# Where a masked prefix scan reads its mask: SBUF rows written by ScalarE, or six features in a PSUM bank written by VectorE

## The chip, the core and the metric

The kernel runs on one NeuronCore of a Trainium2 chip. The metric is the time of one execution on the device in microseconds (us), the median of several runs. TensorE (PE in the profile; PEld is its weight load), VectorE (DVE), ScalarE (ACT), GpSimd (POOL) and SyncE (SP) are the engines. GpSimd issues the indirect DMAs, SyncE and ScalarE issue the plain ones.

## What is computed

A node state x of 12500 rows with 32 features goes through four graph layers. Each layer reads, for every one of 400000 edges, the row of the source node, turns it into a message of 32 features, adds up the messages of each destination node, adds the result to x and normalizes:

```python
edge_index = jnp.stack([src, dst])
...
x = _layernorm(x + _L3_gnn_ref(x, edge_weight, edge_attr_3, edge_index, ...w1, b1, w2, b2), axis=-1)

def _L3_gnn_ref(features, abs_distances, rel_vec, edge_index, w1, b1, w2, b2):
    R = jax.nn.relu(abs_distances[:, None] @ w1 + b1) @ w2 + b2
    Y = spherical_harmonics(rel_vec)
    Fj = features[src]
    ...  # acc += NORM * einsum('euv,ef,evi,ofi->euo', R, Y, Fj, C)
    out = out.at[dst].add(msg)
```

The edges are sorted by destination. So the sum per destination is made as a running sum along the edges that is set back to zero wherever the destination changes: `so[t] = mask[t] * so[t-1] + si[t]`, with a mask of zeros and ones. The last value of every run of equal destinations is the sum of that node.

## The kernel before

Each of the 128 partitions holds 3125 consecutive edges, worked through in 125 chunks of T = 25 edges. The last layer (L3) runs in `vector_edges3`, `scalar_edges3`, `tensor_edges3`, `gpsimd_edges3` and `sync_edges3`, one software pipeline in which every engine has its own hand-written order and waits on counters of the others. The body of a loop holds four chunks, because rows that are gathered have four buffers.

What happens to one chunk c:

- GpSimd (L1937) gathers the source rows, 25 indirect DMAs of one row per partition each, into one of four buffers `gb`. It waits until SyncE's index load is there and until VectorE has begun chunk c-4 (`mA0`).
- VectorE turns the vector part of the gathered rows into the edge's frame with three products `al0`, `al1`, `al2` (L1047), one chunk ahead; TensorE adds the three up with identity matmuls (`along`, L1743) into the PSUM area `L3.rot`, columns 2728 to 3328 of all PSUM, that is from column 168 of bank 5 into bank 6. ScalarE copies the result out (`scalar_split3`, L1427 to L1431).
- TensorE makes the edge's radial weights, 384 numbers per edge, in ten groups of three and two edges: `radial(g)`, L1756. VectorE multiplies each group with the rotated features in two instructions, `mA{g}` and `mB{g}` (L1077 and L1080 for groups 0 to 2, L1087 and L1090 for groups 3 to 9). Groups 0 to 2 are added up by TensorE (`over_v`, L1783), groups 3 to 9 by VectorE (`r3` to `r9`, L1099). `radial(g)` waits for `mB{g-2}`, since its PSUM banks are read by it; so `radial(2)` waits for `mB0`, and `radial(0)` and `radial(1)` of the next chunk for `mB8` and `mB9`. A product waits for its `radial`.
- In the following chunk the sums are turned back: VectorE `bk0`, `bk1`, `bk2` (L1053), TensorE `back` (L1743) into the same `L3.rot`, ScalarE copies them into the scan's input `si` (`scalar_vectors3`, L1443) and counts that in `ac_B`. `si` is stored feature by feature, 32 rows of 26: the first of the 26 is the carried value of the last chunk, copied by ScalarE (L1437), then 25 edges.
- VectorE scans (`sc`, L1156): one instruction over 832 elements per partition, with the mask `L3.mrf`, the same 26 values repeated for the 32 features, as its first input and `si` as its second. Both are in SBUF. The mask row is written by ScalarE once per chunk (L1466, 800 elements), the first column of each 26 is zero from the start (L1161).
- ScalarE turns the scan's output around (`scalar_row3`, L1457) and stores it; then it copies the sums of `over_v` (L1449, L1450), and only after that the split of the next chunk. TensorE's `along(0)` waits for L1450.

The order on VectorE is written out as a list of names; the counter `dv` counts them, and all waits on VectorE are made from the list (`v3(c, name)`). The names in `BACK3` belong to the previous chunk. TensorE's order is radial 0, 1, 2, back 0, radial 3, 4, back 1, radial 5, back 2, radial 6, over_v 0 and 1, radial 7, over_v 2 and 3, radial 8, along 0 and 1, radial 9, along 2. ScalarE's order in a chunk is L1437, L1438, L1466, L1414, L1443, L1420, L1457, L1449, L1450, L1427 to L1431.

Layers 0 and 2 use the same scan on 832 elements, with the mask in PSUM (L847 and L1009); their gathers are L1955 and L1977.

Of the kernel before, what the change touches and what calls it, by code (L numbers as in the profile page):

```python
# [9 lines left out]
ALU = mybir.AluOpType  # L10
ACT = mybir.ActivationFunctionType
# [3 lines left out]
P = 128  # L15
TP = E // P
NP, NJ = 125, 100
T = 25
# [48 lines left out]
def gnn_kernel(nc, x, src, dst, ea2, ea3, ea5, ew, ew1, W0, W1, G2, MU, SG, ROOT, BIAS, w1, b1, w2, b2, out):  # L67

    ctx = ExitStack()
    with ctx:  # L70
        ctx.enter_context(nc.allow_non_contiguous_dma(reason="small strided loads of weights and block heads"))

        def sb(name, shape, dt=F32):
            return ctx.enter_context(nc.sbuf_tensor("s_" + name, shape, dt))
# [6 lines left out]
        def sem(name):  # L81
            if name not in sems:
                sems[name] = ctx.enter_context(nc.semaphore("m_" + name))
            return sems[name]
# [14 lines left out]
        mask = sb("mask", [P, TP])  # L99
# [48 lines left out]
        ps = [psall[:, 512 * i:512 * i + 512] for i in range(8)]  # L148

        dv = Count(sem("dv"))  # L150
        idle = sem("idle")
        idle2 = sem("idle2")
        mk = {}
# [20 lines left out]
        r3 = lambda a: a[0:NP, :].rearrange("p (j c) -> p j c", c=32)  # L174
# [4 lines left out]
        cv = Carve()  # L179
        dsti, dstf, q2 = cv(TP, I32), cv(TP), cv(TP)  # L180
        cv = Carve(17900)
# [12 lines left out]
        for layer in (0, 2):  # L194
            cv = Carve(15400 if layer == 0 else 0)
# [4 lines left out]
        cv = Carve(10350)  # L200
# [23 lines left out]
        cv = Carve()  # L224
# [12 lines left out]
        cv = Carve()  # L237
# [28 lines left out]
        cv = Carve()  # L266
# [19 lines left out]
        cv = Carve()  # L286
# [11 lines left out]
        cv = Carve(21400)  # L298
# [10 lines left out]
        cv = Carve()  # L309
# [22 lines left out]
        cv = Carve()  # L332
        L3 = Layer()
# [2 lines left out]
        L3.fr = [cv(T * 9) for _ in range(2)]  # L336
        L3.HS = [cv(P * T) for _ in range(2)]
        L3.ds = [cv(P * T) for _ in range(2)]
        L3.sif, L3.sof, L3.mrf = ([cv(32 * (T + 1)) for _ in range(2)] for _ in range(3))
        L3.si, L3.so, L3.mr = ([a.rearrange("p (f t) -> p f t", f=32) for a in b] for b in (L3.sif, L3.sof, L3.mrf))  # L340
        L3.sit = [a[:, :, 1:T + 1].rearrange("p f t -> p t f") for a in L3.si]
        L3.row = [cv(32 * T), agg[:, 1800:2600]]
        L3.prod = [cv(3 * 512).rearrange("p (t c) -> p t c", t=3) for _ in range(2)]
# [670 lines left out]
        def vector_edges2(e):  # L1014
# [12 lines left out]
            for k in range(B2):  # L1027
# [3 lines left out]

        ORDER = ("mA0 mB0 mA1 mB1 bk0 mA2 mB2 bk1 mA3 mB3 bk2 mA4 mB4 r3 mA5 mB5 r4 al0 mA6 mB6 r5 sc al1 "
                 "mA7 mB7 r6 al2 mA8 mB8 r7 mA9 mB9 r8 r9").split()
        PER3 = len(ORDER)
        AT3 = {name: n + 1 for n, name in enumerate(ORDER)}
        BACK3 = ("bk0", "bk1", "bk2", "sc")

        def v3(c, name):  # L1040

            return c * PER3 + (mk["base3"] + AT3[name])
# [13 lines left out]
        def vector_chunk3(e, c, i, k, first=False, last=False):  # L1056
            s2, p2 = k % 2, (k - 1) % 2
            R = psall[:, :].rearrange("p (b c) -> p b c", c=512)
            done = lambda name: e.wait_ge(dv.h, v3(c, name))
            done_before = lambda name: e.wait_ge(dv.h, v3(c - 1, name))  # L1060

            def skip(name):
                done(ORDER[AT3[name] - 2])
                e.sem_inc(dv.up(1), 1)

            def prod(g):
                return L3.prod[ONDVE.index(g) % 2][:, 0:GROUPS[g][1]]

            def mul(g):
                t0, n = GROUPS[g]  # L1070
                Rg = R[:, BANK[g]:BANK[g] + n]
                if g == 0:
                    e.wait_ge(sem("ac_G"), c + 1)
                    e.wait_ge(sem("pe_v"), c + 1)
                e.wait_ge(sem("pe_r"), c * 10 + (g + 21))
                if g in ONPE:
                    e.tensor_tensor(  # L1077
                        L3.prodA[:, t0:t0 + n], Rg[:, :, 0:256].rearrange("p t (v b) -> p t v b", v=16),
                        L3.G[s2][:, t0:t0 + n].unsqueeze(3).to_broadcast([P, n, 16, 16]), ALU.mult).then_inc(dv.up(), 1)
                    e.tensor_tensor(  # L1080
                        L3.prodE[:, 2 * t0:2 * (t0 + n)], Rg[:, :, 256:384].unsqueeze(2).to_broadcast([P, n, 2, 128]),
                        L3.GE[s2][:, t0:t0 + n].rearrange("p t a v -> p (t a) v").unsqueeze(3).to_broadcast([P, 2 * n, 16, 8]), ALU.mult).then_inc(dv.up(), 1)
                    return
                pr = prod(g)
                m = ONDVE.index(g)
                done(f"r{ONDVE[m - 2]}") if m > 1 else done_before(f"r{ONDVE[6 - m]}")
                e.tensor_tensor(  # L1087
                    pr[:, :, 0:256].rearrange("p t (b v) -> p t b v", v=16), Rg[:, :, 0:256].rearrange("p t (b v) -> p t b v", v=16),
                    L3.G[s2][:, t0:t0 + n].unsqueeze(2).to_broadcast([P, n, 16, 16]), ALU.mult).then_inc(dv.up(), 1)
                e.tensor_tensor(  # L1090
                    pr[:, :, 256:512], Rg[:, :, 256:384].unsqueeze(2).to_broadcast([P, n, 2, 128]),
                    L3.GE[s2][:, t0:t0 + n].rearrange("p t a v -> p (t a) v").unsqueeze(2).to_broadcast([P, 2 * n, 8, 16]), ALU.mult).then_inc(dv.up(), 1)

            def red(g):
                t0, n = GROUPS[g]
                done(f"mB{g}")
                if g == ONDVE[0]:
                    e.wait_ge(sem("ac_B"), c + 1)
                e.tensor_reduce(L3.sums[s2][:, t0:t0 + n].rearrange("p t c -> p (t c)"),  # L1099
                                prod(g).rearrange("p t (b v) -> p (t b) v", v=16), AX.X, ALU.add).then_inc(dv.up(), 1)  # L1100

            def along(j):
                if last:
                    skip(f"al{j}")
                    return
                if j == 0:
                    e.wait_ge(sem(f"g3_{(k + 1) % 4}"), nth4(i, k + 1) * 400)
                    e.wait_ge(sem("ac_M"), c + 2)
                    e.wait_ge(sem("pe_a"), c + 1)
                along3(e, k + 1, j).then_inc(dv.up(), 1)  # L1110

            def back(name):
                if first:
                    skip(name)
                else:
                    vector_back3(e, c, k, name)

            mul(0)
            mul(1)
            back("bk0")  # L1120
            mul(2)
            back("bk1")
            mul(3)
            back("bk2")
            mul(4)
            red(3)
            mul(5)
            red(4)
            along(0)
            mul(6)  # L1130
            red(5)
            back("sc")
            along(1)
            mul(7)
            red(6)
            along(2)
            mul(8)
            red(7)
            mul(9)
            red(8)  # L1140
            red(9)

        def vector_back3(e, c, k, name):

            s2, p2 = k % 2, (k - 1) % 2
            if name in ("bk0", "bk1", "bk2"):
                if name == "bk0":
                    e.wait_ge(dv.h, v3(c - 1, "r9"))
                    e.wait_ge(sem("ac_V"), c + 1)
                    e.wait_ge(sem("pe_b"), c + 1)  # L1150
                back3(e, k - 1, int(name[2])).then_inc(dv.up(), 1)
            else:
                e.wait_ge(dv.h, v3(c - 1, "sc"))
                e.wait_ge(sem("ac_B"), c + 2)
                e.wait_ge(sem("rowc3"), c)
                e.tensor_tensor_scan(L3.sof[p2], L3.mrf[p2], L3.sif[p2], 0.0, ALU.mult, ALU.add).then_inc(dv.up(), 1)  # L1156

        def vector_ready3(e):
            for a in range(2):
                e.memset(L3.sof[a], 0.0).then_inc(dv.up(), 1)  # L1160
                e.memset(L3.mr[a][:, :, 0:1], 0.0).then_inc(dv.up(), 1)  # L1161

                e.memset(L3.HS[a][64:128], 0.0).then_inc(dv.up(), 1)
                after(e)
                e.memset(L3.HS[a][64:65], 1.0).then_inc(dv.up(), 1)
            after(e)

        def vector_edges3(e):
# [16 lines left out]
            n = 0  # L1185
            for name in BACK3:
                e.wait_ge(dv.h, mk["base3"] + 125 * PER3 + n)
# [275 lines left out]
        def scalar_chunk3(e, c, i, k, first=False, last=False):  # L1463
            if not first:
                scalar_part3(e, c, k)
            e.activation(L3.mr[k % 2][:, :, 1:T + 1], mask[:, bass.ds(c * T, T)].unsqueeze(1).to_broadcast([P, 32, T]), ACT.Copy)  # L1466
            if not last:
                scalar_hidden3(e, i, k + 1, c + 1)
            if not first:
                scalar_vectors3(e, c, k)  # L1470
            if not last:
                e.wait_ge(dv.h, v3(c, "bk2"))
                scalar_frames3(e, i, k + 1)
            if not first:
                scalar_row3(e, c, i, k)
            scalar_sums3(e, c, k)
            if not last:
                scalar_split3(e, c + 1, k + 1)
# [786 lines left out]
```

## Time and profile before

| | us |
|---|---|
| median of 3 runs | 17409.68 |
| lowest and highest run | 17409.63 to 17410.06 |
| profiled execution | 17404.72 |
| its span, first to last instruction | 17402.7 |

One execution is profiled, all engines at once. The busy time of an engine is the sum of its instructions; a row of the timeline gives the start, the duration and, in square brackets, how long the engine was idle before it and what released it. Where several instructions of one line follow each other they stand in one row with xN. PEclk is the granted clock of TensorE as a share of 2.4 GHz; behind it stand the share of the DMA engines and GB/s. Because successive instructions of VectorE overlap a little, the distance from start to start is what one instruction costs in a row of them, and it is a little less than its duration. The last layer's loop takes about 4050 us of the span, from 13184 to 17240.

### The profile page before, as it was taken

To read this page: it belongs to the slowest core of one execution; us is meant where nothing else is said; L and a number is where in the kernel's file an instruction comes from. 1 tells how busy PE (TensorE), PEld (TensorE's weight loads), DVE (VectorE), ACT (ScalarE), POOL (GpSimd) and SP (SyncE) were. 2 spreads that over 40 slices of the span, in tenths; PEclk is the share of its full clock that TensorE was granted. 3 is DMA by queue.
4 is the path that set the end of the run, shared out by engine and by line. 5 is a ranking of instruction groups with operands and counts; after the bars stand their busy time and mean duration, and the time that the engine had idled before them with its cause. 6 is when DMAs were issued, how large, how long until landed. Compare 5 with 4: busy or idle time off the path is not lost. (4 is left out here: it accounts for less than half of the span.)

```text
span 17402.7 us, 138752 instructions
## 1 busy us (share of the span) xinstructions
PE 6419.3 (37%) x33487; PEld 5142.6 (30%) x33487; DVE 12117.7 (70%) x15588; ACT 3285.1 (19%) x5336; POOL 12932.6 (74%) x13715
## 2 busy tenths in 40 slices
PE   1000000000444454545330000000006999999995
PEld 0000000000333333333320000000005878878774
DVE  5666666674899999999663232223326999999996
ACT  0000000000222222222541101111102223222321
POOL 6777777777677777777757777777777777777776
PEclk9555555555777777777665555555558999999998
DMA  4333333331111111111332222222222222222221
GB/s 103 97 96 97 97 98 97 98 97 47 28 28 28 28 28 28 28 28 25 130 130 59 59 57 59 58 59 58 59 53 45 55 55 53 56 53 56 53 56 36
DMA packets 744244, 1076.69 MB, mean 62 GB/s; under 512 B 375703, under 2 KB 508493, under 8 KB 731294
## 3 DMA queue, kind: packets, MB, share of 16 engines
q0 software_dynamic: 417376, 477.82, 12.5%
q1 hardware_dynamic: 250851, 398.14, 8.2%
q10 hardware_dynamic: 75736, 197.70, 3.1%
q8 instruction: 88, 1.44, 0.0%
q14 instruction: 193, 1.58, 0.0%
HBM read 684.92 MB, written 389.48 MB: 62 GB/s over the span
## 5 line engine op out<-in xcount | busy, mean ns | idle before, releaser
L1937 POOL DMA_INDIRECT s_arena<-d_t,s_arena x3125 | 3086.5, 988 | 971.3 <-issue 943.6
L1898 POOL DMA_INDIRECT d_pay<-s_arena x3125 | 3026.9, 969 | 997.7 <-issue 931.0
L1977 POOL DMA_INDIRECT s_arena<-d_t,s_arena x3125 | 2960.6, 947 | 1032.6 <-issue 952.0
L1955 POOL DMA_INDIRECT s_arena<-d_t,s_arena x3125 | 2948.5, 944 | 981.7 <-issue 952.1
L1649 PE MATMUL psall<-s_arena 128*128 128x500 bf16 x1875 | 835.4, 500 | 4365.4 <-DVE psall L881 3637.1
L992 DVE TENSOR_TENSOR s_arena<-s_arena,psall 128x2400 f32<-128x2400 f32 x125 | 332.0, 2656 | 2712.1 <-DMA s_arena<-d_t,s_arena 2712.1
L1649 PEld LDWEIGHTS psall<-s_arena 128*128 128x128 bf16 x1875 | 222.5, 119 | 4783.3 <-DVE psall L881 3708.7
L1756 PE MATMUL psall<-s_w2r,s_arena 128*128 128x384 f32 x4250 | 1514.0, 491 | 5.9 <-DVE s_arena L1090 5.2
L1838 PE MATMUL psall<-s_tails,s_mfix 128*128 128x32 f32 x6 | 1.9, 412 | 3972.8 <-DVE s_tails L1198 3972.8
L1756 PEld LDWEIGHTS psall<-s_w2r,s_arena 128*128 128x128 f32 x4250 | 1271.0, 317 | 64.3 <-DVE s_arena L1090 6.1
L1099 DVE TENSOR_REDUCE s_arena<-s_arena 128x64 f32<-128x1024 f32 x875 | 1248.1, 1438 | 0.0
L1838 PEld LDWEIGHTS psall<-s_tails,s_mfix 128*128 128x128 f32 x6 | 1.5, 313 | 3974.0 <-DVE s_tails L1198 3974.0
L1666 PE MATMUL psall<-s_ident,s_arena 128*128 128x128 f32 x3125 | 603.3, 321 | 1406.8 <-DVE s_arena L665 1406.8
L1675 PE MATMUL psall<-s_arena 128*128 128x128 f32 x6250 | 1052.1, 316 | 112.3 <-ACT s_arena L1360 103.5
L901 DVE TENSOR_REDUCE s_arena<-s_arena 128x600 f32<-128x4200 f32 x125 | 1027.2, 8218 | 4.3
L1360 ACT ACTIVATE s_arena<-psall 128x512 f32<-128x512 f32 x875 | 482.7, 552 | 2743.3 <-PE psall L1666 2743.3
L1675 PEld LDWEIGHTS psall<-s_arena 128*128 128x128 f32 x6250 | 906.0, 221 | 309.7 <-DVE s_arena L688 150.6
L564 DVE TENSOR_TENSOR s_arena<-s_arena,psall 128x625 bf16<-128x625 f32 x1250 | 957.7, 801 | 0.0
L890 DVE TENSOR_TENSOR s_arena<-s_arena,psall 128x600 f32<-128x600 f32 x125 | 97.5, 780 | 1172.4 <-DMA s_arena<-d_t,s_arena 1172.4
L1783 PE MATMUL psall<-s_arena,s_ident 128*128 128x256 f32 x4000 | 907.4, 378 | 0.0
L1666 PEld LDWEIGHTS psall<-s_ident,s_arena 128*128 128x128 f32 x3125 | 451.9, 168 | 1430.0 <-issue 1430.0
L1512 ACT ACTIVATE s_arena<-s_arena 128x800 f32<-128x800 f32 x125 | 213.9, 1711 | 3492.9 <-DVE psall L864 3463.7
(304 smaller groups left out, 17923.9 us busy)
## 6 DMA issues: line engine op xcount, KB each, us to landing
s_arena<-d_t,s_arena POOLq DMA_INDIRECT x9375, 2.5
d_scan<-s_arena ACTq DMA_DIRECT2D x313, 400.0 KB, 2.6
s_arena<-d_ew SPq DMA_DIRECT2D x126, 800.0 KB
s_arena<-d_pay SPq DMA_DIRECT2D x33, 1650.0 KB, 6.8
d_inj<-s_agg SPq DMA_DIRECT2D x125, 400.0 KB, 3.9
s_arena<-d_inj SPq DMA_DIRECT2D x125, 400.0 KB, 3.4
d_pay<-s_arena POOLq DMA_INDIRECT x3125, 2.2
d_fold<-s_arena ACTq DMA_DIRECT2D x33, 1250.0 KB, 4.9
```

The lines of the kernel that those rows point to most:

```text
L564: return e.tensor_tensor(O[sl], h5[:, :, bass.ds(n, 1)].to_broadcast([P, 5, 125]), iob, ALU.is_equal)
L901: e.tensor_reduce(S[:, :, 8:32], w7.rearrange("p m t c -> p t c m"), AX.X, ALU.add)
L1099: e.tensor_reduce(L3.sums[s2][:, t0:t0 + n].rearrange("p t c -> p (t c)"), prod(g).rearrange("p t (b v) -> p (t b) v", v=16), AX.X, ALU.ad ...
L1649: e.matmul(R5s[:, 0:4], lhsT, rhs[:, 0:4], start=start, stop=True, skip_group_check=True)
L1666: m = e.transpose(ps[6][:, 128 * t:128 * t + 128], S1.xb[:, 128 * (t0 + t):128 * (t0 + t) + 128], ident[:, :])
L1675: m = e.matmul(ps[2 + yb][:, 128 * t:128 * t + 128], S1.xT[yb][:, 128 * t:128 * t + 128], S1.wt, start=True, stop=True)
L1756: m = e.matmul(ps[BANK[g] + t][:, 0:384], hv_[:, :, t0 + t], L3.w2v if g in ONPE else w2r[:, :], start=True, stop=True)
L1783: m = e.matmul(L3.vs, ident[:, :], L3.prodP[:, v], start=v == 0, stop=v == 15, skip_group_check=True)
L1898: e.indirect_dma_start(pay_d, bass.IndirectOffsetOnAxis(ap=S1.adr[s4][:, t:t + 1], axis=0), S1.pay[s4][:, 33 * t:33 * t + 33], None).then_ ...
L1937: e.indirect_dma_start(L3.gb[s][:, t], None, T3_d, bass.IndirectOffsetOnAxis(ap=L3.idx[s][:, t:t + 1], axis=0)).then_inc(sem(f"g3_{s}"), 16)
L1955: e.indirect_dma_start(L0.gb[s][:, t * 128:(t + 1) * 128], None, T0_d, bass.IndirectOffsetOnAxis(ap=L0.idx[s][:, t:t + 1], axis=0)).then_i ...
L1977: e.indirect_dma_start(L2.gb[k][:, t * 96:(t + 1) * 96], None, T2_d, bass.IndirectOffsetOnAxis(ap=L2.idx[k][:, t:t + 1], axis=0)).then_inc ...
```

## The change

VectorE gets a new step `mk`, placed ahead of `r4`. It copies the 25 mask values of the chunk, repeated for six features, from SBUF into columns 0 to 155 of PSUM bank 5, which nothing used. The mask of ScalarE (L1466) and both SBUF mask buffers are gone. The scan `sc` becomes six instructions, five of 156 elements and one of 52, each with the same PSUM mask; it moves from behind `r5` to ahead of `al0`. The wait on `ac_B`, which stood at `sc`, now stands at `mk`. For the first chunk there is a memset of the six zero columns instead of `mk`.

```diff
-        L3.sif, L3.sof, L3.mrf = ([cv(32 * (T + 1)) for _ in range(2)] for _ in range(3))
+        L3.sif, L3.sof = ([cv(32 * (T + 1)) for _ in range(2)] for _ in range(2))
+        L3.mrf = ps[5][:, 0:6 * (T + 1)]
+        L3.mr = L3.mrf.rearrange("p (f t) -> p f t", f=6)
...
-        ORDER = ("mA0 mB0 mA1 mB1 bk0 mA2 mB2 bk1 mA3 mB3 bk2 mA4 mB4 r3 mA5 mB5 r4 al0 mA6 mB6 r5 sc al1 "
+        ORDER = ("mA0 mB0 mA1 mB1 bk0 mA2 mB2 bk1 mA3 mB3 bk2 mA4 mB4 r3 mA5 mB5 mk r4 sc al0 mA6 mB6 r5 al1 "
                  "mA7 mB7 r6 al2 mA8 mB8 r7 mA9 mB9 r8 r9").split()
-        BACK3 = ("bk0", "bk1", "bk2", "sc")
+        BACK3 = ("bk0", "bk1", "bk2", "mk", "sc")
...
             mul(5)
+            if first:
+                e.wait_ge(sem("ac_B"), c + 2)
+                e.memset(L3.mr[:, :, 0:1], 0.0).then_inc(dv.up(), 1)
+            else:
+                back("mk")
             red(4)
+            back("sc")
             along(0)
             mul(6)
             red(5)
-            back("sc")
             along(1)
...
-            else:
+            elif name == "mk":
+                at = (c - 1) * T
+                m = mask[:, at:at + T] if isinstance(c, int) else mask[:, bass.ds(at, T)]
                 e.wait_ge(dv.h, v3(c - 1, "sc"))
                 e.wait_ge(sem("ac_B"), c + 2)
+                e.tensor_copy(L3.mr[:, :, 1:T + 1], m.unsqueeze(1).to_broadcast([P, 6, T])).then_inc(dv.up(), 1)
+            else:
+                e.wait_ge(dv.h, v3(c, "mk"))
                 e.wait_ge(sem("rowc3"), c)
-                e.tensor_tensor_scan(L3.sof[p2], L3.mrf[p2], L3.sif[p2], 0.0, ALU.mult, ALU.add).then_inc(dv.up(), 1)
+                for f in range(0, 32, 6):
+                    a, b = f * (T + 1), min(f + 6, 32) * (T + 1)
+                    m = e.tensor_tensor_scan(L3.sof[p2][:, a:b], L3.mrf[:, 0:b - a], L3.sif[p2][:, a:b], 0.0, ALU.mult, ALU.add)
+                m.then_inc(dv.up(), 1)
...
-            e.activation(L3.mr[k % 2][:, :, 1:T + 1], mask[:, bass.ds(c * T, T)].unsqueeze(1).to_broadcast([P, 32, T]), ACT.Copy)
```

## Rows read from the trace of the kernel before

**Rows 1.** Stretch: us, busy (count) of PE, PEld, DVE, ACT, POOL; PEclk.

```profile
15000.00:16000.00 1000.00, 941.10 (x3286) 800.74 (x3285) 944.59 (x1054) 298.74 (x434) 764.33 (x774) 0.98 0.25 55
```

**Rows 2.** Gathers of layers 3 and 2: calls, busy us, mean ns, idle.

```profile
L1937 POOL DMA_INDIRECT s_arena<-d_t,s_arena x3125 | 3086.5, 988 | 971.3 <-issue 943.6
...
L1977 POOL DMA_INDIRECT s_arena<-d_t,s_arena x3125 | 2960.6, 947 | 1032.6 <-issue 952.0
```

**Rows 3.** Timeline: one scan, and the gather that starts beside it.

```profile
15021.93 1.88 DVE L1156 TENSOR_TENSOR_SCAN s_arena<-s_arena 128x832 f32<-128x832 f32 x1
...
15022.22 2.35 POOL L1937 DMA_INDIRECT s_arena<-d_t,s_arena  x1 [0.30 <-issue]
```

**Rows 4.** VectorE's timeline of one undisturbed chunk, mA0 to the next mA0.

```profile
15003.96 0.95 DVE L1077 TENSOR_TENSOR s_arena<-psall,s_arena 128x768 f32<-128x768 f32 x1
...
15008.20 0.96 DVE L1077 TENSOR_TENSOR s_arena<-psall,s_arena 128x768 f32<-128x768 f32 x1 [0.54 <-PE psall L1756]
...
15016.73 1.74 DVE L1099 TENSOR_REDUCE s_arena<-s_arena 128x96 f32<-128x1536 f32 x1
...
15023.73 0.76 DVE L1047 TENSOR_TENSOR s_agg<-s_arena,psall 128x600 f32<-128x600 f32 x1
...
15027.26 0.77 DVE L1047 TENSOR_TENSOR s_agg<-s_arena,psall 128x600 f32<-128x600 f32 x1
...
15031.35 0.69 DVE L1087 TENSOR_TENSOR s_arena<-psall,s_arena 128x512 f32<-128x512 f32 x1 [0.38 <-PE psall L1756]
...
15035.34 0.95 DVE L1077 TENSOR_TENSOR s_arena<-psall,s_arena 128x768 f32<-128x768 f32 x1
```

**Rows 5.** Timeline, ScalarE and TensorE: L1443, along 2, radial 2.

```profile
15015.78 1.35 ACT L1443 ACTIVATE s_arena<-psall 128x600 f32<-128x600 f32 x1 [7.33 <-PE psall L1743]
...
15031.06 1.17 PE L1743 MATMUL psall<-s_agg,s_ident 128*128 128x344 f32 x4
...
15037.21 1.52 PEld L1756 LDWEIGHTS psall<-s_ta,s_arena 128*128 128x128 f32 x5 [2.22 <-DVE s_arena L1080]
```

**Rows 6.** Waits in the whole loop: us in total, times, longest.

```profile
ACT s_arena L1443 <- PE psall L1743: 985.1, 125, 10.3
...
DVE s_agg L1047 <- DMA s_arena<-d_t,s_arena: 57.7, 27, 8.5
```

**Rows 7.** Two successive mA0, and a stretch between them.

```profile
14615.64 0.95 DVE L1077 TENSOR_TENSOR s_arena<-psall,s_arena 128x768 f32<-128x768 f32 x1
...
14648.71 0.95 DVE L1077 TENSOR_TENSOR s_arena<-psall,s_arena 128x768 f32<-128x768 f32 x1
...
14619.00:14623.00 4.00, 4.00 (x9) 2.56 (x9) 2.46 (x4) 1.12 (x1) 3.09 (x4) 0.61 0.08 12
```

**Rows 8.** Two copies into PSUM, layer 2's scan, a short scan.

```profile
2030.06 0.23 DVE L863 COPY psall<-s_arena 128x75 f32<-128x75 f32 x1
2030.20 0.20 DVE L864 COPY psall<-s_arena 128x50 f32<-128x50 f32 x1
...
L1009 DVE TENSOR_TENSOR_SCAN s_arena<-psall,s_arena 128x832 f32<-128x832 f32 x125 | 236.6, 1892 | 23.2 <-DVE s_arena L949 4.8 <-DVE s_arena L956 4.6 <-DVE s_arena L972 4.6
...
L581 DVE TENSOR_TENSOR_SCAN s_arena<-s_arena 128x125 f32<-128x125 f32 x1 | 0.4, 420 | 0.0
```

**Rows 9.** The loop's last scan, and the copy it waits for.

```profile
17238.61 1.32 ACT L1443 ACTIVATE s_arena<-psall 128x600 f32<-128x600 f32 x1 [5.02 <-PE psall L1743]
17240.02 1.89 DVE L1156 TENSOR_TENSOR_SCAN s_arena<-s_arena 128x832 f32<-128x832 f32 x1 [4.31 <-ACT s_arena L1443]
```

**Rows 10.** mA0 of chunk 1 and of chunk 124.

```profile
13223.38 0.95 DVE L1077 TENSOR_TENSOR s_arena<-psall,s_arena 128x768 f32<-128x768 f32 x1
...
17201.71 0.95 DVE L1077 TENSOR_TENSOR s_arena<-psall,s_arena 128x768 f32<-128x768 f32 x1
```

**Rows 11.** First and last of 14 gaps over 2.4 us at radial 2.

```profile
13225.24 1.27 PEld L1756 LDWEIGHTS psall<-s_ta,s_arena 128*128 128x128 f32 x4 [2.64 <-DVE s_arena L1080]
...
17203.58 1.84 PEld L1756 LDWEIGHTS psall<-s_ta,s_arena 128*128 128x128 f32 x6 [2.94 <-DVE s_arena L1080]
```

More of the change, by code:

```diff
@@ L338, in gnn_kernel @@
         L3.ds = [cv(P * T) for _ in range(2)]
-        L3.sif, L3.sof, L3.mrf = ([cv(32 * (T + 1)) for _ in range(2)] for _ in range(3))
-        L3.si, L3.so, L3.mr = ([a.rearrange("p (f t) -> p f t", f=32) for a in b] for b in (L3.sif, L3.sof, L3.mrf))
+        L3.sif, L3.sof = ([cv(32 * (T + 1)) for _ in range(2)] for _ in range(2))
+        L3.si, L3.so = ([a.rearrange("p (f t) -> p f t", f=32) for a in b] for b in (L3.sif, L3.sof))
+        L3.mrf = ps[5][:, 0:6 * (T + 1)]
+        L3.mr = L3.mrf.rearrange("p (f t) -> p f t", f=6)
         L3.sit = [a[:, :, 1:T + 1].rearrange("p f t -> p t f") for a in L3.si]
@@ L1160, in vector_ready3 @@
                 e.memset(L3.sof[a], 0.0).then_inc(dv.up(), 1)
-                e.memset(L3.mr[a][:, :, 0:1], 0.0).then_inc(dv.up(), 1)
                 e.memset(L3.HS[a][64:128], 0.0).then_inc(dv.up(), 1)
```

## The prediction

> **What bounds the kernel now.** I went from the stretches to the timeline of one chunk, and from there to the waits. In the middle of the loop TensorE is busy for 94.1% and VectorE for 94.5% of the time, ScalarE for 30% [rows 1]. GpSimd shows 76%, but it never rests: its gathers are 0.30 us apart ("issue") and wait for nobody. So three engines are nearly full, and the change touches two of them.
>
> GpSimd: a gather takes 0.94 us plus 0.30, so 25 of them take about 31.2 us. In layer 3 the mean is 988 ns, in layer 2 it is 947 [rows 2]; 3125 x 41 ns = 128 us of extra. It sits in one place: of the 123 gathers longer than 1 us, 122 lie at a scan. The gather that starts 0.29 us after the scan takes 2.35 us and ends 0.76 us behind it [rows 3]. Layer 2's scan, equally long but with its mask in PSUM, lengthens none. The Trainium skill, "SBUF — State Buffer", section "Who interferes with whom", says that a VectorE instruction with two SBUF inputs holds up a GpSimd instruction that reads SBUF. The trace agrees, by those 122.
>
> TensorE and VectorE: an undisturbed chunk takes 31.38 us from mA0 to mA0 [rows 4]. VectorE is idle twice in it, 0.54 us before mA2 and 0.38 us before mA9, both times for TensorE. TensorE is idle once, 2.22 us, before radial 2, which waits for mB0 [rows 5]. So the loop goes: mB0, then TensorE without a break from radial 2 to radial 9, then VectorE alone with mA9, mB9, r8, r9, mA0, mB0. From mA2 to mA9 VectorE has 0.38 us to spare, not more.
>
> The measured mean is higher: 3978.33 us for 123 chunks [rows 10], 118.6 us above 123 x 31.38 = 3859.7. Two things make it up. After some of the gaps TensorE runs at the lower of its two clocks for a few us: one chunk takes 33.07 us, 1.69 more, with PEclk at 0.61 in a stretch of 4 us in it [rows 7], that is at 1.2 GHz for most of the stretch. I count 42 such starts in 124. The waits bear it out: L1443 waits 7.33 us in the undisturbed chunk [rows 5] and 985.1 in all [rows 6]; less the longest of 10.3, and less 124 x 7.33, that leaves 66 us, or 39 times 1.69. 42 x 1.69 = 71 us. The other 47.6 us are chunks in which al0 waits for the gathered rows (57.7 us in 27 waits, the longest of them ahead of these chunks [rows 6]).
>
> **Part by part.**
> - *ScalarE loses L1466 (0.89 us).* Worth nothing: behind it ScalarE waits 7.33 us for TensorE at L1443 [rows 5].
> - *The wait on ac_B moves up to mk.* L1443 ends at 15015.78 + 1.35 = 15017.13 [rows 5]; at the loop's end the scan starts 0.09 us after that copy is done [rows 9]. So mk starts at 15017.22 where r4 started at 15016.73 [rows 4]: 0.49 us of VectorE standing still. L1443 is fixed by TensorE's back 2, which doesn't move. Behind the wait stand r4, sc, al0 and everything up to mA9. At sc, 5 us later, the same wait cost nothing.
> - *mk, 150 elements, SBUF to PSUM.* The copy of 75 elements costs 0.14 us from start to start [rows 8]; 75 more, at mA2's 0.96 us less the overlap for 768 elements [rows 4], add 0.09. I take 0.22 us. Bounds: 0.14, and 0.31 if it doesn't overlap.
> - *Six pieces for one scan.* The scan of 832 takes 1.88 us, and 1.80 from start to start [rows 3, 4]. Between 125 elements (0.420) and 832 (1.892) [rows 8] an element costs 2.08 ns, which leaves 0.07 us fixed from start to start, or 0.15 as a duration. Five more pieces: 0.33 us, between 0 and 0.75. The mask in PSUM adds 0.01 (1.892 against 1.882).
> - *The pages price the pieces higher.* The trace shows an overlap of 0.08 us between the scan and al1 [rows 3, 4]. The Trainium skill, "VectorE: DVE Perf Modes", section "The DRAIN you can't avoid", says that the next instruction doesn't start until the pipe is empty, and advises few instructions. By that the pieces cost five full fixed parts; that is the high end above, and a rival below.
> - *sc and mk ahead of al0, mA6, mB6, r5.* al0 comes 0.49 + 0.22 + 2.14 = 2.85 us later, al1 and all behind it 1.05 us later. TensorE has room: al2 ends at 28.03, after the change at 29.1, and along 2 starts at 31.06 [rows 4, 5]; radial 8 and radial 9 have more. ScalarE's L1457 starts some 2.6 us earlier, which helps only where al0 waited for gathers.
> - *GpSimd's stall goes.* 31.2 us a chunk instead of 32.3. Alone it cannot give more than the 47.6 us of gather waits.
> - *SyncE, the DMAs issued and the start of the loop* stay. The tail, where mk and scan stand behind L1443, gets 0.6 us longer.
>
> **The sum.** VectorE gets 0.49 + 0.22 + 0.34 = 1.05 us between mA2 and mA9, has 0.38 to spare, and so mA9, and with it mB0 and the next radial 2, come 0.67 us later: 123 x 0.67 = 82 us. With a chunk now at 32.0 us or more and gathers at 31.2, the gather waits go: 47 us less. And TensorE's gap grows from 2.22 to 2.9 us. The gaps over 2.4 us that the trace has are 14 [rows 11], and after 7 of them the clock fell; of the 110 others 35 did. From 0.32 at 2.22 us and 0.5 at about 2.56 (most of the 14) a straight line gives 0.67 at 2.9: 83 starts instead of 42, 41 x 1.69 = 69 us. In all 82 - 47 + 69 + 1 = 105 us. The profiled execution took 17404.7 (span 17402.7); that gives 17510, and since the median of the runs is 5 us above the profiled one, 17515.
>
> **The rivals.**
> 1. *The clock falls no oftener.* Then 82 - 47 + 1 = 36 us, 17446 (each rival's time likewise against the median). For it: rows 11 are few. Against it: their share is above that of the short gaps. Chance 0.14; it lies on the border between no change and slower.
> 2. *VectorE pays each piece in full, or nearly every start runs slow.* Pieces at 0.15: 0.49 + 0.31 + 0.76 = 1.56, less 0.38 is 1.18, times 123 = 145; the clock falls in nearly all, 80 x 1.69 = 135; less 47: 233 us, 17643. The page named above would have it so for the first half. Against it: all rows of VectorE overlap. Chance 0.14.
> 3. *Faster: the added work fits into the spare time.* If mk does not have to wait and the pieces cost nothing, VectorE gets 0.22 to 0.38 us, mA9 stays where it is, and GpSimd's freed port shows in full: 47 us less, 17363. The place is mA9; the point from which it decides is an addition of 0.38 us. With mk unhindered but the pieces at 0.33 the addition is 0.56, the loop 0.18 longer, the clock a few times slower: 22 - 47 + 20, no change. For it: three causes of lost time (port, ScalarE, late scan) are truly taken away. Against it: mk's wait ends by TensorE's order. Chance 0.12 for faster, 0.08 for the middle.
> 4. *The gathers are still held up,* by mk instead of the scan, since it too reads SBUF. Layer 0's copies into PSUM (L863, L864) lengthen no gather. It would hardly show: 32.3 us of GpSimd is still below the 33 of the loop. No time of its own.
>
> **How the numbers follow.** Forecast 0.52, rival 1 0.14, rival 2 0.14, rival 3 and its middle 0.20. About 0.2% (35 us) is what a measurement can tell: faster means below 17375, slower above 17445. Faster 0.12; no change 0.08 plus half of rival 1, 0.15; slower the rest, 0.73. The forecast's own range, with mk at 0.14 to 0.31 us and 0.5 to 0.85 of the starts slow, is 17471 to 17563: 73 us for VectorE and 34 for 62 starts at the low end, 93 and 106 (105 starts) at the high end, less 47, plus 1. For eight in ten the range goes from 17390, leaving out only rival 3's faster part, to 17620, leaving out the end of rival 2.
>
> **What would show it.** In the profile of the changed kernel: gathers of layer 3 at a mean of 944 to 947 ns; GpSimd waiting for VectorE's mA0 (chunk c-4), which it never did; no DMA wait at al0 after the first chunks; mk idle 0.4 to 0.5 us for L1443; pieces 0.39 us apart; no idle before mA9; TensorE's gap at radial 2 of 2.9 us; undisturbed chunks of 32.0 us, slow ones of 33.7, and PEclk in the loop at 0.96 rather than 0.98. The forecast is wrong if mk starts at once, if mA9 still waits for TensorE, or if the gap grows and the slow starts don't.

## The result and the profile after

The changed kernel takes 17545.83 us (median of 4 runs, 17545.06 to 17549.53) against 17409.72 us of the kernel before on the same chip: a ratio of 1.0078, interval 1.0066 to 1.0090, 136 us slower. The profiled execution takes 17545.06 us, its span is 17543.0. The forecast was 105 us slower.

The middle of the loop by stretch, with the columns of [rows 1]:

```profile
15000.00:16000.00 1000.00, 928.49 (x3178) 780.58 (x3179) 926.44 (x1198) 262.52 (x388) 704.85 (x748) 0.96 0.25 53
```

All engines are less busy than before, and TensorE's mean clock is 0.96 instead of 0.98. The gathers, the pieces and the copy as groups:

```profile
L1950 POOL DMA_INDIRECT s_arena<-d_t,s_arena x3125 | 2948.6, 944 | 1216.5 <-issue 918.6
...
L1170 DVE TENSOR_TENSOR_SCAN s_arena<-psall,s_arena 128x156 f32<-128x156 f32 x620 | 243.2, 458 | 0.0
L1164 DVE COPY psall<-s_mask 128x150 f32 x120 | 38.2, 318 | 56.6 <-ACT s_arena L1457 56.6
```

A gather now takes 944 ns instead of 988 [rows 2], so the time that the scan took from GpSimd is gone (3086.5 - 2948.6 = 138 us). mk waited 56.6 us in 120 times, 0.47 us each. (L1457 is the copy that was L1443; L1769 is `radial`, L1756 the turns, L1079 and L1082 mA and mB of groups 0 to 2, L1089 those of the others.) The waits of the loop:

```profile
PEld psall L1769 <- DVE s_arena L1082: 366.4, 125, 3.6
...
POOL s_arena L1950 <- DVE s_arena L1089: 167.7, 61, 4.3
...
DVE s_arena L1079 <- issue: 14.2, 29, 0.7
DVE s_agg L1049 <- DMA s_arena<-d_t,s_arena: 8.4, 1, 8.4
```

GpSimd, which never waited, now waits (the line above alone is 167.7 us). The view names VectorE, since GpSimd waits on two semaphores there and VectorE's counter moved last. The timeline shows that the other one, SyncE's load of the chunk's indices, is what GpSimd waits for:

```profile
15015.37 0.34 SPq L2119 DMA_DIRECT2D s_arena<-in_src  x1
...
15022.26 0.94 POOL L1950 DMA_INDIRECT s_arena<-d_t,s_arena  x1 [2.30 <-DVE s_arena L1089]
```

The gather starts 6.89 us after the load was issued. From chunk 5 on the first gather of a chunk comes late 107 times, and each time it starts 6.4 to 8.1 us after its index load, while the mA0 of chunk c-4 lies more than 55 us back. SyncE in turn issues the load only after a wait for ScalarE (L1434, 123 times, 31.6 us each). So GpSimd is paced by the loop through ScalarE and SyncE, and not through its four buffers.

VectorE's waits for gathers have gone from 27 to the one at the start [rows 6]. TensorE's gap at radial 2 is 366.4 / 125 = 2.93 us in the mean. One line is new: VectorE stands still before mA0 in 29 chunks, for nothing that the profile shows. One undisturbed chunk on the timeline:

```profile
15011.81 1.36 ACT L1457 ACTIVATE s_arena<-psall 128x600 f32<-128x600 f32 x1 [9.86 <-PE psall L1756]
...
15012.16 0.68 DVE L1092 TENSOR_TENSOR s_arena<-psall,s_arena 128x512 f32<-128x512 f32 x1
15013.32 0.32 DVE L1164 COPY psall<-s_mask 128x150 f32 x1 [0.48 <-ACT s_arena L1457]
15013.54 1.74 DVE L1101 TENSOR_REDUCE s_arena<-s_arena 128x96 f32<-128x1536 f32 x1
...
15015.20 2.12 DVE L1170 TENSOR_TENSOR_SCAN s_arena<-psall,s_arena 128x156 f32<-128x156 f32 x6
...
15017.24 0.75 DVE L1049 TENSOR_TENSOR s_agg<-s_arena,psall 128x600 f32<-128x600 f32 x1
...
15027.97 0.69 DVE L1089 TENSOR_TENSOR s_arena<-psall,s_arena 128x512 f32<-128x512 f32 x1
...
15033.83 1.66 PEld L1769 LDWEIGHTS psall<-s_ta,s_arena 128*128 128x128 f32 x5 [2.81 <-DVE s_arena L1082]
```

The instruction ahead of r4 in the chunk of [rows 4], mB5, was this one:

```profile
15016.14 0.68 DVE L1090 TENSOR_TENSOR s_arena<-psall,s_arena 128x512 f32<-128x512 f32 x1
```

mk starts 0.15 us after L1457 is done. The bracket gives 0.48 us of idle time, but from start to start mB5 to mk takes 1.16 us where mB5 to r4 took 0.59, so the wait costs 0.57 us: the overlap of two instructions is lost with it. mk costs 0.22 us from start to start; the six pieces take 2.04 us from start to start where one scan took 1.80 [rows 3, 4]; mA9 (15027.97) no longer waits; and TensorE's gap is 2.81 us where it was 2.22 [rows 5]. The slow start that follows it is the rule now. The first and the last mA0 of the 123 chunks of [rows 10]:

```profile
13226.50 0.95 DVE L1079 TENSOR_TENSOR s_arena<-psall,s_arena 128x768 f32<-128x768 f32 x1
...
17339.21 0.95 DVE L1079 TENSOR_TENSOR s_arena<-psall,s_arena 128x768 f32<-128x768 f32 x1
```

That is 4112.7 us, 134.4 more than before. An undisturbed chunk takes 31.97 us (0.59 more), a slow one 33.65; 98 of 123 are slow. The sum: 123 x 0.59 = 73 us, 56 more slow starts x 1.68 = 94, the new stops 14, less the 48 us of gather waits: 133.

### The profile page after: what moved, and what is told of

Read it like the earlier page. It is cut to its first block and busy times, and to the rows that moved or that the text cites. A ratio compares the mean times of both kernels' runs of the same rounds, so it can differ in the third digit from the quotient of the medians.

```text
span 17543.0 us, 139502 instructions
## 1 busy us (share of the span) xinstructions
PE 6494.2 (37%) x33487; PEld 5167.4 (29%) x33487; DVE 12184.8 (69%) x16337; ACT 3180.3 (18%) x5211; POOL 12796.6 (73%) x13715
## 5 line engine op out<-in xcount | busy, mean ns | idle before, releaser
L1950 POOL DMA_INDIRECT s_arena<-d_t,s_arena x3125 | 2948.6, 944 | 1216.5 <-issue 918.6
L1990 POOL DMA_INDIRECT s_arena<-d_t,s_arena x3125 | 2960.9, 947 | 1032.9 <-issue 952.1
L1968 POOL DMA_INDIRECT s_arena<-d_t,s_arena x3125 | 2948.6, 944 | 982.5 <-issue 952.1
L1769 PE MATMUL psall<-s_w2r,s_arena 128*128 128x384 f32 x4250 | 1510.4, 490 | 5.8 <-DVE s_arena L1092 5.2
L1769 PEld LDWEIGHTS psall<-s_w2r,s_arena 128*128 128x128 f32 x4250 | 1274.8, 317 | 58.1 <-DVE s_arena L1092 6.1
L1769 PE MATMUL psall<-s_ta,s_arena 128*128 128x384 f32 x2000 | 837.5, 569 | 304.8 <-DVE s_arena L1082 304.8
```

The source lines that it names most:

```text
L1769: m = e.matmul(ps[BANK[g] + t][:, 0:384], hv_[:, :, t0 + t], L3.w2v if g in ONPE else w2r[:, :], start=True, stop=True)
L1950: e.indirect_dma_start(L3.gb[s][:, t], None, T3_d, bass.IndirectOffsetOnAxis(ap=L3.idx[s][:, t:t + 1], axis=0)).then_inc(sem(f"g3_{s}"), 16)
L1968: e.indirect_dma_start(L0.gb[s][:, t * 128:(t + 1) * 128], None, T0_d, bass.IndirectOffsetOnAxis(ap=L0.idx[s][:, t:t + 1], axis=0)).then_i ...
L1990: e.indirect_dma_start(L2.gb[k][:, t * 96:(t + 1) * 96], None, T2_d, bass.IndirectOffsetOnAxis(ap=L2.idx[k][:, t:t + 1], axis=0)).then_inc ...
```

## Experiments

Two things were to be told apart: whether VectorE's added time alone, with TensorE's slower starts behind it, makes the 136 us, or something in the new form (mask, port, wait, pieces); and whether the slow starts really come from the length of TensorE's gap. Times are medians, each against the kernel before as it was measured beside it (17402.8 to 17411.8); gains are counted from there too. A chunk's kind and the slow starts are counted over the 123 chunks from mA0 to mA0; a fall of the clock in a chunk that waits for gathers is not counted as a slow start.

**1. Only time added.** The kernel before with one useless instruction:

```diff
             mul(5)
+            e.memset(L3.pad, 0.0)      # 1150 elements
             red(4)
```

> The kernel before with one idle instruction on VectorE ahead of r4, a memset of 1150 elements, about 1.05 us, and nothing else: no mk, no pieces, no wait, no PSUM mask. My theory: this alone gives the change's result but for its loop turn (14 us): undisturbed chunks 32.0 us, TensorE's gap 2.8 to 2.9 us, some 98 slow starts, no gather waits, 73 + 92 - 48 = +117 us against the kernel before. Rival B (the time added counts, the slow starts stay at 42): +25. Rival D (GpSimd's long gathers, which stay here, add to it): over +150.

Measured: 17541.36 us against 17402.83, ratio 1.0080 (1.0064 to 1.0097), 139 us. That is the change's ratio with none of its parts. The groups and the wait:

```profile
L1129 DVE MEMSET s_arena<- 128x1150 f32 x125 | 127.1, 1017 | 23.5 <-issue 23.5
...
L1939 POOL DMA_INDIRECT s_arena<-d_t,s_arena x3125 | 3011.1, 964 | 1154.1 <-issue 925.7 <-DVE s_arena L1088 123.4 <-DVE s_agg L1048 66.4
```

The memset brought 0.19 us of idle time with it, so VectorE got 1.13 us instead of 1.05 (from mB5 to al0, start to start, median of the undisturbed chunks), and an undisturbed chunk takes 32.10: 123 x 0.72 = 89 us, 98 slow starts, (98 - 42) x 1.68 = 94, less 48: 135. The gathers are still held up by the scan (964 ns) and GpSimd waits all the same: rival D is out, and so is B. That the result comes within 3 us of the change's is in part luck, since this kernel has no stops before mA0 and 0.13 us more in each chunk. Its gap at radial 2 is also shorter, 2.57 us in the mean, and TensorE stands idle a second time, ahead of along 0:

```profile
15018.47 1.89 PEld L1745 LDWEIGHTS psall<-s_agg,s_ident 128*128 128x128 f32 x8 [0.62 <-issue]
```

**2. The gap of TensorE filled.** Four matmuls of the identity (eight in a second run) behind radial 1, into columns 384 to 511 of a bank whose other columns radial 1 has just written; nobody reads them. Radial 1's count goes up behind them:

```diff
                     m = e.matmul(ps[BANK[g] + t][:, 0:384], hv_[:, :, t0 + t], ...)
+                if g == 1:
+                    for _ in range(4):
+                        m = e.matmul(ps[BANK[g] + n - 1][:, 384:512], ident[:, :], ident[:, :], start=True, stop=True, ...)
                 m.then_inc(sem("pe_r"), 1)
```

> The changed kernel with four extra 128x128 matmuls of the identity into unused columns of a PSUM bank behind radial 1, where TensorE stands idle; nothing reads them. My theory: the idle gap falls below 2 us, no chunk starts at the lower clock, and although TensorE does more work the time falls by nearly 98 x 1.68 = 165 us, to 17385. Rival C (the extra 1.7 us of the slow chunks comes from something else, such as loads or DMA): no gain, 17546 or more, since only work is added.

> The changed kernel with eight idle-time matmuls behind radial 1 instead of four, which left a gap of 1.76 us and 20 slow starts. My theory: the gap falls to about 0.7 us, the slow starts go altogether, 20 x 1.68 = 34 us less than with four: 17379. Rival E (the extra matmuls get in the way of mA1 or radial 2): no less than with four, 17413 or more.

> The kernel before with the same four idle-time matmuls. My theory: the slow starts go here too (42 x 1.69 = 71 us), but GpSimd's gathers at 32.3 us a chunk then are the bound, VectorE waits for gathers instead, and the time stays at 17410, at best 10 us less. If GpSimd were no bound before: 17340. Rival C: 17410 or more without any more gather waits.

Measured: the changed kernel with four 17412.74, with eight 17382.15 (0.9984, 0.9974 to 0.9993), the kernel before with four 17412.96 (1.0005, 0.9996 to 1.0015). The changed kernel, 136 us above the kernel before, is 9 above it with four matmuls and 30 below it with eight: by doing more work it gets 127 and 166 us back. Its slow starts are 98, 20 and 0, and all of the 20 lie in the 29 chunks that begin with a stop before mA0. The stretch and the gap, first with four, then with eight:

```profile
15000.00:16000.00 1000.00, 950.62 (x3521) 823.95 (x3520) 954.21 (x1236) 272.70 (x401) 728.55 (x773) 0.99 0.24 55
...
PEld psall L1769 <- DVE s_arena L1082: 218.1, 124, 2.4
```

```profile
15000.00:16000.00 1000.00, 978.03 (x3804) 856.94 (x3803) 962.27 (x1246) 276.58 (x406) 735.37 (x779) 1.00 0.25 55
...
PEld psall L1769 <- DVE s_arena L1082: 108.5, 124, 1.6
```

The mean gap is 1.76 and 0.87 us, and the granted clock goes from 0.96 to 0.99 and 1.00 of 2.4 GHz. In the kernel before the same fill gains nothing, since there the gathers bind:

```profile
DVE s_agg L1047 <- DMA s_arena<-d_t,s_arena: 128.9, 61, 8.2
```

VectorE waits 128.9 us for gathers where it waited 57.7 [rows 6]: what the clock gave was taken by GpSimd at 32.3 us a chunk. The clock still falls in 19 chunks there, all of them chunks of 35.7 us and more that wait for gathers.

**3. The mask in SBUF.** The changed kernel with `L3.mrf = cv(6 * (T + 1))` instead of the PSUM columns.

> The changed kernel with its mask of six features in SBUF instead of PSUM, everything else kept. My theory (VectorE's added time and TensorE's slower starts set the loop, GpSimd has room): the gathers beside the scans get long again, GpSimd's waits for mA0 shrink by as much, and the time stays at that of the changed kernel, 17546 us within 0.1%. Rival A (GpSimd's port is what the loop depends on): slower than the changed kernel, by up to 128 us, 17670.

Measured: 17526.06 us, ratio 1.0070 (1.0054 to 1.0087), not to be told from the changed kernel's 1.0078. The gathers, though, did not go back to 988:

```profile
L1950 POOL DMA_INDIRECT s_arena<-d_t,s_arena x3125 | 2970.7, 951 | 1184.3 <-issue 916.5 <-DVE s_arena L1089 154.7 <-DVE s_agg L1049 53.4
```

They lose 7 ns each and not 44: the cut into pieces frees nearly all of the port, the place of the mask the rest. I had expected them to be long again. An undisturbed chunk takes 31.91 us, and 95 are slow.

**4. The wait where it costs nothing.** The mask needs no wait on `ac_B` when it isn't in the bank that L1457 reads. On top of experiment 3:

```diff
             elif name == "mk":
                 e.wait_ge(dv.h, v3(c - 1, "sc"))
-                e.wait_ge(sem("ac_B"), c + 2)
...
             else:
                 e.wait_ge(dv.h, v3(c, "mk"))
+                e.wait_ge(sem("ac_B"), c + 2)
```

> As the one before (mask of six in SBUF), and the wait on ac_B moved from mk back to sc, behind r4, where it should cost nothing. My theory: VectorE gets 0.57 us a chunk instead of 1.05, an undisturbed chunk 31.5 instead of 31.97, TensorE's gap 2.35 instead of 2.81, and starts at the lower clock fall from 98 to about 55: 123 x 0.48 + 43 x 1.68 = 131 us less, 17415. Rival B (the slower starts don't depend on the length of the gap): only the 59 us of the wait, 17487. Rival A: no faster than the changed kernel.

Measured: 17401.36 us, ratio 0.9999 (0.9989 to 1.0008). The wait is worth 125 us against experiment 3, about twice its own price: an undisturbed chunk takes 31.38 us instead of 31.91, 123 x 0.53 = 65 us, and 58 are slow instead of 95, 37 x 1.68 = 62. With the mask in bank 5, where part of `L3.rot` lies, which ScalarE is reading at that moment, moving the wait was not tried.

**5. Both cures together.** Experiment 4 with the four matmuls.

> The mask of six in SBUF, the wait on ac_B at sc, and the four idle-time matmuls behind radial 1, all three together. My theory: 31.5 us a chunk, 0.11 more for the loop turn, hardly a slow start, gathers (31.4 us a chunk) just below: 3978 us of the loop before become 123 x 31.6 = 3887 and some 20 for what is left of slow starts, -70 us, 17334. Rival A (GpSimd binds again, as in the kernel before with the fill): -20 at best.

Measured: 17308.75 us, ratio 0.9946 (0.9930 to 0.9963), 94 us faster than before; one slow start is left.

**6. Only the pieces.** The kernel before, its mask still written by ScalarE into SBUF, its order untouched, the scan cut in six:

```diff
-                e.tensor_tensor_scan(L3.sof[p2], L3.mrf[p2], L3.sif[p2], 0.0, ALU.mult, ALU.add).then_inc(dv.up(), 1)
+                for f in range(0, 32, 6):
+                    a, b = f * (T + 1), min(f + 6, 32) * (T + 1)
+                    m = e.tensor_tensor_scan(L3.sof[p2][:, a:b], L3.mrf[p2][:, a:b], L3.sif[p2][:, a:b], 0.0, ALU.mult, ALU.add)
+                m.then_inc(dv.up(), 1)
```

> The kernel before, its mask in SBUF written by ScalarE and the scan behind r5 as it was; only the scan is cut into six pieces. My theory: 0.33 us more on VectorE, which mA9's 0.38 us of waiting takes up, so an undisturbed chunk stays at 31.4; the gathers are held up by a piece at most, as in the run with the SBUF mask (mean 951 ns instead of 988), so the gather waits go (-48 us); the loop turn costs 14, slow starts rise from 42 to about 48 (+10): -24 us in all. Rival A (only an input in PSUM frees the port): the gathers stay at 988 and the time is +14 or more.

> The one before with the four idle-time matmuls. My theory: no slow starts and no gather waits, 31.4 us a chunk and 0.11 for the loop turn: 123 x 31.5 = 3875 instead of 3978, -100 us, 17304, the fastest of all. Rival A: GpSimd binds at 32.3 us a chunk, no gain. Rival C (the fill works only where the gap is above 2.8 us): -24, as without it.

> The fastest so far (mask in SBUF from ScalarE, scan in pieces, four idle-time matmuls) with two pieces of 416 elements instead of six. My theory: what holds a gather is the length of one piece, now 0.98 us, so the gathers' mean lies between 951 (six pieces) and 988 (one), near 965, GpSimd at 31.6 to 31.8 a chunk binds, and the time is 25 to 50 us above the 17291 of six pieces. Rival F (any cut frees the port, whatever the length): 951 ns and 17291 or a little less.

Measured: six pieces 17363.70 us (0.9978, 0.9968 to 0.9987), 39 us faster than before; with the four matmuls 17291.24 (0.9936, 0.9920 to 0.9953), 112 us faster than before and 248 faster than the change; two pieces with the matmuls 17296.28 (0.9933, 0.9917 to 0.9950), the same. Without the matmuls the undisturbed chunks take 31.4 us: mA9's spare time took up the five extra pieces, and there are 47 slow starts, and no stop before mA0, which I had put at 14 us. With the matmuls 122 of 123 chunks take 31.3 to 31.4 us. Two pieces at 950 ns a gather beat my expectation of 965. The timeline of the kernel with two pieces and the matmuls shows why:

```profile
15008.42 1.93 DVE L1158 TENSOR_TENSOR_SCAN s_arena<-s_arena 128x416 f32<-128x416 f32 x2
15009.08 1.10 POOL L1943 DMA_INDIRECT s_arena<-d_t,s_arena  x1 [0.30 <-issue]
```

The gather beside the two pieces is 0.16 us late and ends before the second piece does. The first piece alone takes 1.01 us, to 15009.43, and the gather ends 0.75 us behind it, just as a gather ends 0.75 us behind the whole scan in the kernel before [rows 3]: it was held by the first piece and not by the second. GpSimd waits for nothing in this kernel, and 6 ns a gather, or 0.15 us a chunk, is the same figure again. A hit at a random moment would cost more. One reason would fit, but no run tests it: 25 free gathers take 31.2 us against the loop's 31.38, so GpSimd gains on the scan until the hold makes up the difference.

**7. Where the stops before mA0 come from.** The kernel before with twelve memsets of one column each ahead of r4.

> The kernel before with twelve memsets of one column per chunk on VectorE, ahead of r4, to see whether the wait at the loop's turn (0.4 to 0.7 us before every fourth mA0, with 339 packets on the instruction queue instead of 193) comes from the length of VectorE's loop body. If so, both appear here: 29 waits before mA0, 339 packets or more, and with 0.8 us of added time 17404 + 52 + 60 - 48 + 14 = 17482. If it comes from something else in mk (its address is computed each time), the queue stays at 193 and every turn is without a wait.

Measured in one run: 17405.56 us, no change (17411.84 the median before). The stops are there, 29 of them, on the page as 339 packets of the instruction queue; the kernel before and the six pieces of experiment 6 have 193 and 194 and no stop:

```profile
q14 instruction: 339, 2.78, 0.1%
```

So they come with the length of VectorE's loop body and not with mk. Twelve memsets take 0.21 us together, not the 0.8 I had put down, and leave the chunk at 31.38. Stops and 55 slow starts use up what were gather waits, so that the time stays.

## Why the prediction was right

The direction, the range and the mechanism hold; the forecast of 105 us is 31 short of 136. By its steps:

- *ac_B's wait at mk.* Forecast 0.49 us. The idle time measured is 0.47 to 0.48, the cost from start to start 0.57. Experiment 4 shows that it is the dearest part of the change.
- *mk.* Forecast 0.22 us, measured 0.22 from start to start.
- *Six pieces.* Forecast 0.34 us more with the mask in PSUM, measured 2.04 - 1.80 = 0.24. The sentence of the Trainium skill, "VectorE: DVE Perf Modes", section "The DRAIN you can't avoid", that the prediction took for its high end (0.75 in all), is not the whole of that section: it adds that a next instruction that is not held starts earlier. That is what the trace shows, pieces of 0.46 us that start 0.37 us apart.
- *mA9's spare 0.38 us taken up, the loop longer by the rest.* Forecast 0.67 us, measured 0.59: 73 us for 82. VectorE got 0.57 + 0.22 + 0.24 = 1.03 us, close to the forecast 1.05 only because the wait was dearer and the pieces were cheaper, two errors that nearly cancel. And it had more to spare: 0.35 us at mA9 and 0.08 ahead of mA8, a wait too short for a bracket, which the prediction had not counted. Experiment 1 gets the same result from time alone.
- *The gather waits go.* Forecast 47 us less, measured 48. GpSimd waits instead, though not for mA0 of chunk c-4, as the prediction said, but for SyncE's index load. Experiment 2 shows by the kernel before that GpSimd did bind there.
- *TensorE's slower starts.* The straight line from two kinds of gap gave 83, the runs show 98: 94 us instead of 69. This is the term that was mis-sized. Of the 98, 29 are the chunks that begin with a stop; their gap is 3.3 to 3.6 us and every one of them is slow. Of the other 94, with 2.8 us, 69 are: 0.73, against the forecast 0.67 at 2.9. So the line was fair, and some 10 of the 15 starts too many come from the stops, which the sum did not have. That idle time of TensorE is the cause is shown by experiment 2; experiments 1 and 4 give its sign in both directions. The length of this one gap is not the whole measure: experiment 1 has the same 98 at 2.57 us, with TensorE idle a second time.
- *Not foreseen:* the stops at the loop's turn, 14 us by themselves and about 16 more by the slow starts behind them. The count of instructions per loop body went up, and I had costed that at nothing.
- *GpSimd's port.* The cause was right as far as it went. Experiment 6 shows that it was worth having only together with an unchanged VectorE, and that the cut alone gives it; the mask in PSUM, which brought the wait and mk, was not needed.
- *ScalarE's L1466* was worth nothing, as forecast: experiment 6 keeps it and is the fastest of all.
- *Rival 1* (slow starts stay at 42) falls by the count, rival 2 by the pieces' price, and by 98 slow starts where it had nearly all 123, rival 3 by mk's wait, rival 4 by 944 ns.

## What to carry to other kernels

When two engines hand a loop back and forth, look for the one wait that is left on the longer engine before moving work to it: here VectorE had some 0.4 us to spare in 31.38, and every tenth above it came back doubled, because TensorE's idle gap grew and more of its starts ran at 1.2 GHz. If a gap of TensorE is paid for twice, useless matmuls in it can be cheaper than the gap (166 us here), as long as no other engine binds just behind. And a cure for one bound (the gathers' port) should be tried alone, in its cheapest form, before it is bundled with what it costs.

## What the runs showed of the hardware

- A gather that starts beside a scan with two inputs in SBUF is held until that instruction ends, not until a whole row of them does, and ends 0.75 us behind it: 988 ns in the mean with one scan of 832 elements, 950 with two of 416, 951 to 954 with six, 944 with the mask in PSUM.
- Memsets of one column cost 0.0175 us each in a row of twelve (0.21 us), far less than the 0.07 us fixed that larger instructions show.
- A loop body of VectorE beyond some length brings a stop of 0.4 to 0.7 us at each turn of the loop, and 339 packets on the instruction queue instead of 193. Five more scans per chunk don't bring it; five more scans and mk, or twelve memsets, do. Where between them the limit lies was not tried.
- How often the clock falls to 1.2 GHz behind TensorE's gap at radial 2 (the 94 are the chunks that no stop precedes, the lengths are medians): none of 94 at 1.6 us (experiment 2, four matmuls), 34 of 94 and 47 of 123 at 2.2 us (experiments 4 and 6), 66 of 94 at 2.75 us (experiment 3), 69 of 94 at 2.8 and 29 of 29 at 3.3 to 3.6 us (the changed kernel). Equal gaps don't fare alike: behind a stop 20 of 29 starts are slow with four matmuls in front of a gap of 2.1 to 2.4 us (experiment 2), and in the kernel with six pieces the slow starts come every second or third chunk, and no run shows what picks them.
